# Opening of a two-layer adaptive FFN kernel: bias as two fp32r products, a subtraction on GpSimd, an earlier load, conversions behind additions, one low rank product sooner

## The reference, cut to what matters

```python
att = softmax(gelu(gelu(cond @ W0 + b0) @ W1 + b1) @ W2 + b2)      # 64 x 8
agg_w = einsum('bk,koi->boi', att, weight)                         # 64 x 32 x 32
agg_b = att @ bias_k                                               # 64 x 32
c = einsum('boi,bih->boh', agg_w, x) + agg_b[:, :, None]

def qlinear(x, q, scale, A, Bm):
    w = (q - 7.5) * (scale * 0.005)[:, None]
    return x @ w.T + 0.02 * (x @ A @ Bm)                           # A: 512 x 32, Bm: 32 x 1376
h = silu(qlinear(c, gate...)) * qlinear(c, up...)
x = x + qlinear(h, down...)
x = x + ffn_fp8(conv(x) + context)
```

## Time and profile before

| | us |
|---|---|
| median of three runs | 390.03 (390.01 to 390.49) |
| the profiled execution | 390.28 |
| its span, first to last instruction | 388.4 |
| TensorE busy | 376.7 (97%) |
| VectorE busy | 253.5 (65%) |
| ScalarE busy | 167.6 (43%) |
| GpSimd busy | 80.1 (21%) |

### The profile page before, as it was taken

One profiled execution on the slowest core, in us unless ns is written; L12 is line 12 of the kernel. 1 busy time (PEld: TensorE's weight loads), 2 busy tenths in 40 slices (PEclk: granted clock), 3 DMA queues, 4 the chain that ended last, 5 costly groups with the idle time before them and its releaser, 6 DMA issues.

```text
span 388.4 us, 5833 instructions
## 1 busy us (share of the span) xinstructions
PE 376.7 (97%) x2249; PEld 310.2 (80%) x2249; DVE 253.5 (65%) x406; ACT 167.6 (43%) x304; POOL 80.1 (21%) x67
## 2 busy tenths in 40 slices
PE   7999999999999999999999999999999999999894
PEld 3776877899888888998888789988888899996341
DVE  2659888827376665363766653647889732697994
ACT  6436698402255553022555540225666500254122
POOL 2001422411123223111233231112332312000000
PEclk9699999999999999999999999999999999999999
DMA  6798564199320000222200002254000499974235
GB/s 217 251 278 278 176 217 163 31 323 183 45 43 0 0 2 1 41 42 40 42 0 3 1 0 42 42 70 119 2 0 1 127 294 226 167 187 86 83 136 218
DMA packets 81964, 40.53 MB, mean 104 GB/s; under 512 B 52344, under 2 KB 72840, under 8 KB 81808
## 3 DMA queue, kind: packets, MB, share of 16 engines
q1 hardware_dynamic: 69280, 37.80, 37.0%
q10 hardware_dynamic: 12480, 1.56, 2.7%
q0 software_dynamic: 176, 0.79, 0.6%
HBM read 26.38 MB, written 13.75 MB: 103 GB/s over the span
## 4 chain that ended last, share of the span: by engine, by line
PE 82%; ACT 7%; DVE 7%; issue 2%; POOL 1%; DVEq 0%; ACTq 0%
PE ps L605 34%; PE ps L594 21%; PE ps L541 4%; PE ps L615 4%; PE ps L636 4%; PE ps L770 3%; PE ps L750 2%; PE ps L670 2%; PE ps L638 2%; PE ps L550 1%; DVE y_buf L1102 1%; ACT a_buf L894 1%; ACT mix L834 1%; ACT b_buf L897 1%; PE ps L502 1%
## 5 line engine op out<-in xcount | busy, mean ns | idle before, releaser
L963 POOL TENSOR_TENSOR h_lo<-a_buf,h_hi 128x512 fp32r<-128x512 f32 (+1 forms) x44 | 57.5, 1307 | 126.4 <-ACT h_hi L867 126.4
L594 PE MATMUL ps<-down_w,h_hi 128*128 128x288 f32 (+1 forms) x352 | 76.9, 300 | 0.4 <-DVE down_w L1021 0.3
L594 PE MATMUL ps<-down_w,h_lo 128*128 128x288 f32 (+1 forms) x352 | 74.8, 294 | 0.0
L605 PE MATMUL ps<-x_hi,gate_w 128*128 128x512 f32 (+1 forms) x176 | 70.0, 398 | 0.1
L605 PE MATMUL ps<-x_hi,up_w 128*128 128x512 f32 (+1 forms) x176 | 69.7, 396 | 0.1
L605 PE MATMUL ps<-x_lo,gate_w 128*128 128x512 f32 (+1 forms) x176 | 69.5, 395 | 0.0
L605 PE MATMUL ps<-x_lo,up_w 128*128 128x512 f32 (+1 forms) x176 | 69.3, 394 | 0.0
L1229 DVE TENSOR_TENSOR a_buf<-a_buf,b_buf 128x512 f32<-128x512 f32 (+1 forms) x44 | 54.2, 1233 | 11.6 <-ACT a_buf L908 9.8
L594 PEld LDWEIGHTS ps<-down_w,h_hi 128*128 128x128 f32 (+1 forms) x352 | 57.3, 189 | 1.9 <-issue 0.8
L594 PEld LDWEIGHTS ps<-down_w,h_lo 128*128 128x128 f32 (+1 forms) x352 | 56.2, 188 | 0.0
L1224 DVE TENSOR_TENSOR b_buf<-ps,b_buf 128x512 f32<-128x512 f32 (+1 forms) x44 | 30.2, 686 | 18.9 <-ACT b_buf L897 14.6
(11 more groups left out here) (172 smaller groups left out, 454.6 us busy)
## 6 DMA issues: line engine op xcount, KB each, us to landing
x_nat<-in_x SPq DMA_DIRECT2D x4, 1024.0 KB, 7.7
out<-x_nat SPq DMA_DIRECT2D x16, 256.0 KB, 2.2
turned<-x_nat SPq DMA_DIRECT2D x12, 256.0 KB, 3.3
x_nat<-in_down_q SPq DMA_DIRECT2D x11, 256.0 KB, 3.0
x_nat<-in_gate_q SPq DMA_DIRECT2D x10, 256.0 KB, 7.1
x_nat<-in_up_q SPq DMA_DIRECT2D x10, 256.0 KB, 8.4
edges<-zeros SPq DMA_DIRECT2D x4, 512.0 KB, 9.6
xt<-turned SPq DMA_DIRECT2D x6, 256.0 KB, 3.7
```

Source lines behind the costliest of these rows:

```text
L594: last = mm(ps[:, 4 + 2 * (j % 2) + m, 0:HALF + R], part[0:k, ic, j * P:(j + 1) * P], down_w[0:k, ic, m, :], start=first, stop=end)
L605: last = mm(ps[0:k, bank(ic, 2 * m), :], w[:, H * ic + c * k:H * ic + (c + 1) * k], part[:, c, :], start=c == 0 and part is x1_hi, stop=c ...
L963: nc.gpsimd.tensor_tensor(h_lo[0:k, ic, :], a_buf[0:k, ic % 2, :], plain(h_hi[0:k, ic, :]), ALU.subtract).then_inc(h_lo_ready, 1)
```

## The change

Five edits, all in the opening and the first tile.

1. The bias product is made of fp32r operands. ScalarE rounds `att_bias` to `att_bias_hi` and the ones to `ones_r`; VectorE makes `att_bias_lo`; TensorE adds two one-pass products in the same bank. The 16 passes for the mixture have one `keep_clock` product among them in place of three, and four in place of one stand ahead of `condition(0)`.
2. The low part of B (128 x 688) is subtracted by GpSimd in place of VectorE.
3. The load of `sel` is issued ahead of SP's wait for the parts of B.
4. The two conversions of each chunk of tile 0 stand behind the two additions.
5. The first low rank product stands ahead of the last feature chunk of the third gate product.

```diff
@@ -133,13 +133,16 @@
         bias_k_sb = sb("bias_k_sb", [EXPERTS, S], F32, early)
         cond_w_sb = sb("cond_w_sb", [EXPERTS, S // OB, P], F32, early)
         att_bias = sb("att_bias", [EXPERTS, TILE // S, S], F32, early)
+        att_bias_hi = sb("att_bias_hi", [EXPERTS, TILE], F32R, early)
+        att_bias_lo = sb("att_bias_lo", [EXPERTS, TILE], F32R, early)
+        ones_r = sb("ones_r", [EXPERTS, P], F32R, early)
         stage_lr_a = sb("stage_lr_a", [P, HC, 2, R], F32, early)
         stage_sel = sb("stage_sel", [P, P], F32, early)
         stage_mask = sb("stage_mask", [P, GROUPS + P], F32, early)
         stage_side = sb("stage_side", [P, S], F32, early)
         stage_ctx_w = sb("stage_ctx_w", [P, S], F32, early)
 
-        used = 4 * (COND_COLS + 2 * B + 3 * EXPERTS + B + 6 + S + S // OB * P + TILE + HC * 2 * R + P
+        used = 4 * (COND_COLS + 2 * B + 3 * EXPERTS + B + 6 + S + S // OB * P + 3 * TILE + P + HC * 2 * R + P
                     + GROUPS + P + S + S)
         pad_h = sb("pad_h", [P, (4 * IC * TILE - used) // 4 + 32], F32, early)
         stage_lr_b = sb("stage_lr_b", [P, 2, LRC], F32, early)
@@ -222,6 +225,7 @@
         mix_mm = sem("mix_mm")
         mix_ready, mix_saved, mix_rest = sem("mix_ready"), sem("mix_saved"), sem("mix_rest")
 
+        bias_hi, bias_lo = sem("bias_hi"), sem("bias_lo")
         aggb_mm, aggb_ready = sem("aggb_mm"), sem("aggb_ready")
         row_mm, row_ready, row_stored, row_in = sem("row_mm"), sem("row_ready"), sem("row_stored"), sem("row_in")
 
@@ -410,6 +414,7 @@
             sp.dma_start(stage_ctx_w[:], ctx_w).then_inc(ctx_in, 16)
             sp.dma_start(stage_side[:], fside).then_inc(ctx_in, 16)
             sp.dma_start(stage_mask[:], batch_mask).then_inc(ctx_in, 16)
+            sp.dma_start(stage_sel[:], sel_in).then_inc(sel_w_in, 16)
             sp.wait_ge(lrb_hi, 1)
             sp.wait_ge(lrb_ready, 1)
             sp.dma_start(lr_b_rows.rearrange("m v r (c n) -> (r c) m v n", n=LRC),
@@ -422,7 +427,6 @@
                              lr_b_rows.rearrange("m v r n -> (v r) m n")).then_inc(lrb_laid, 16)
             for n in range(6, RING):
                 load_slot(n)
-            sp.dma_start(stage_sel[:], sel_in).then_inc(sel_w_in, 16)
             sp.dma_start(down_sb[:], down_s).then_inc(down_in, 16)
             sp.dma_start(stage_down_a[:].rearrange("p c r -> p (c r)"), down_a).then_inc(down_in, 16)
             sp.dma_start(stage_down_b[:], down_b).then_inc(down_in, 16)
@@ -522,13 +526,14 @@
             pe.wait_ge(mixw_in, 2 * 16)
             for o in range(S // OB):
                 last = mm(ps[:, MIX_BANK, o * B:(o + 1) * B], cond_w_sb[:, o, :], att_t[:], start=True, stop=True)
-                if o % 2 == 1 and o < S // OB - 1:
+                if o == S // OB // 2 - 1:
                     keep_clock(1)
             last.then_inc(mix_mm, 1)
 
-            pe.wait_ge(att_ready, 2)
-            mm(ps[:, BIAS_BANK, :], ones[0:EXPERTS, :], att_bias[:].rearrange("k b s -> k (b s)"),
-               start=True, stop=True).then_inc(aggb_mm, 1)
+            pe.wait_ge(bias_hi, 2)
+            pe.wait_ge(bias_lo, 1)
+            mm(ps[:, BIAS_BANK, :], ones_r[:], att_bias_hi[:], start=True, stop=False)
+            mm(ps[:, BIAS_BANK, :], ones_r[:], att_bias_lo[:], start=False, stop=True).then_inc(aggb_mm, 1)
 
             def condition(t):
 
@@ -647,7 +652,7 @@
                               start=False, stop=True)
                 last.then_inc(conv_mm, 1)
 
-            keep_clock(1)
+            keep_clock(4)
             pe.wait_ge(mix_ready, 2)
             condition(0)
 
@@ -697,7 +702,8 @@
                     pe.wait_ge(y_ready, t * TG - 1)
                 if t == 0:
                     pe.wait_ge(ag_ready, 1)
-                    quantised(0, 2, 0)
+                    for c in range(HC - 1):
+                        quantised_chunk(0, 2, 0, c)
                     pe.wait_ge(lrb_laid, 2 * 16)
                 for m in range(2):
                     if t > 0:
@@ -709,6 +715,8 @@
                     if t == 0 and m == 1:
                         pe.wait_ge(ctx_sum, 1)
                     low_rank(t, 0, m)
+                    if t == 0 and m == 0:
+                        quantised_chunk(0, 2, 0, HC - 1)
                 low_rank(t, 1, 0)
                 low_rank(t, 1, 1)
                 for ic in range(2, IC):
@@ -795,6 +803,9 @@
 
             act.wait_ge(lr_in, 2 * 16)
             activation(lr_a_w[:, :, :, 0, :], stage_lr_a[:], copy).then_inc(lra_hi, 1)
+            act.wait_ge(att_ready, 2)
+            activation(att_bias_hi[:], att_bias[:].rearrange("k b s -> k (b s)"), copy).then_inc(bias_hi, 1)
+            activation(ones_r[:], ones[0:EXPERTS, :], copy).then_inc(bias_hi, 1)
             act.wait_ge(lrb_in, 16)
             activation(lr_b_parts[:, :, 0, :], stage_lr_b[:], copy).then_inc(lrb_hi, 1)
             act.wait_ge(mix_mm, 1)
@@ -952,6 +963,9 @@
         def _(pool):
             nc.gpsimd.memset(mix[:], 0.0).then_inc(mix_zero, 1)
             nc.gpsimd.memset(zeros[:], 0.0).then_inc(zero_set, 1)
+            pool.wait_ge(lrb_hi, 1)
+            nc.gpsimd.tensor_tensor(lr_b_parts[:, :, 1, :], stage_lr_b[:], plain(lr_b_parts[:, :, 0, :]),
+                                    ALU.subtract).then_inc(lrb_ready, 1)
             pool.wait_ge(row_ready, 1)
             nc.gpsimd.dma_start(bias_row, row_sb).then_inc(row_stored, 16)
 
@@ -1004,9 +1018,9 @@
             v.tensor_tensor(lr_a_w[:, :, :, 1, :], stage_lr_a[:], plain(lr_a_w[:, :, :, 0, :]),
                             ALU.subtract).then_inc(lra_ready, 1)
 
-            dve.wait_ge(lrb_hi, 1)
-            v.tensor_tensor(lr_b_parts[:, :, 1, :], stage_lr_b[:], plain(lr_b_parts[:, :, 0, :]),
-                            ALU.subtract).then_inc(lrb_ready, 1)
+            dve.wait_ge(bias_hi, 1)
+            v.tensor_tensor(att_bias_lo[:], att_bias[:].rearrange("k b s -> k (b s)"), plain(att_bias_hi[:]),
+                            ALU.subtract).then_inc(bias_lo, 1)
 
             dve.wait_ge(mix_mm, 1)
             dve.wait_ge(mix_zero, 1)
@@ -1213,15 +1227,15 @@
                         down_b_low()
                     if t == 0 and ic == 5:
                         convolution_low()
-                    if t == 0:
-                        for later in range(EARLY + 2 * ic, EARLY + 2 * ic + 2):
-                            convert(later)
                     dve.wait_ge(ag_ready, n + 1)
                     dve.wait_ge(l_mm, 2 * n + 1)
                     v.tensor_tensor(a, ps[0:k, bank(ic, 1), :], a, ALU.add).then_inc(g_ready, 1)
                     dve.wait_ge(au_ready, n + 1)
                     dve.wait_ge(l_mm, 2 * n + 2)
                     v.tensor_tensor(b, ps[0:k, bank(ic, 3), :], b, ALU.add).then_inc(u_ready, 1)
+                    if t == 0:
+                        for later in range(EARLY + 2 * ic, EARLY + 2 * ic + 2):
+                            convert(later)
                     if t == TILES - 1 and ic == W_SPREAD - 1:
                         largest_of(w_row_mm, bank(W_SPREAD, 1), w_max, w_steps)
                     dve.wait_ge(silu_ready, n + 1)
```

## The result

The changed kernel takes 388.32 us at the median of seven runs (386.68 to 389.31), the kernel before, timed beside it, 390.49 (390.01 to 390.74). The ratio is 0.9948, with a 95% interval of 0.9924 to 0.9971: faster, by 2.2 us. Before's times lie within 0.7 us of each other, those of the change within 2.6. The three at 389.2 to 389.3 have a mean granted clock of 0.989, the two at 387.7 and 388.3 have 0.992 and 0.993, the two at 386.7 have 0.996.

A forecast was written before the change was run, and what follows sets the result against it. TensorE's chain of waits was taken as the bound: 1.8 (opening) + 0.8 (low rank and conversions) + 0.2 (after) = 2.8 us off the profiled 390.28, giving 387.5. With the median 0.25 below that execution, 387.3 us; range 386.1 to 388.9.

The forecast's parts named there:

- Start of the mixing at 12.9: Opening, tile 0: with the matrix ready at about 12.8 us, `condition(0)` starts at 12.9, 0.7 us sooner.
- bias pair: Opening on TensorE: two one-pass fp32r products at 0.24 us each, 0.5 in place of 1.51 us, ending at 11.4.
- End of the mixing at 17.9: End of `condition(0)`: middle taken between 19.39 (clock rises at 18.56) and 16.47 (high throughout), gain 1.8 us.
- the late clock: Rival, opening: the clock comes back as late as before; gain 1.3 us, 388.7 us, chance 0.14.
- the rival in which the clock never falls: Rival, opening: no low clock once the slow bias product is gone; gain 3.8 us, 386.2 us, chance 0.12.
- Four products bring the clock back sooner: Opening: TensorE runs full products from 11.4 us with hardly a hole, so the clock should rise sooner; time not known.
- sel, worth nothing alone, and without it the gain is lost: `sel` load issued at 9.2 us lands by about 16; alone worth nothing, here it lets the opening's 1.8 us through.
- B on GpSimd costs nothing: Opening: B's store goes 1.8 us later, second reading lands by 27.5 at worst, cover 2.4 us, cost nothing.
- Low rank and conversions, 0.8 us: First low rank products, tile 0: up product of the third chunk starts at 31.65 instead of 32.43, gain 0.8 us.
- After that, 0.2 gained of a range of 0.3 gained to 0.5 lost: Rest of tile 0's gate stage: later products of halves on VectorE meet a 0.31 us wait; 0.2 us gained taken.
- the vector engines as the bound: Rival, tile 0: ScalarE does not follow and TensorE waits at `down`; 0 to 0.8 us gained, 389.6 us, chance 0.06.
- B too late: Rival, opening: GpSimd's subtraction ends at 21.2 us, TensorE waits for B; loss some 4 us, 394 us, chance 0.02.

The follow-up runs named there:

- 12 further runs: The changed kernel itself, nothing altered, timed again beside the kernel before: 388.02 us at the median, ratio 0.9937.
- change's second profile: Profile from re-timing the unaltered changed kernel beside the kernel before: span 386.2 us; median of those runs 388.02 us.

## Why the prediction was right, and where it was not

The range (386.1 to 388.9) held the median of 388.32 and the side was right. The gain was 2.2 us and not 2.8, the predicted 387.3 lay 1.0 under the median, and the forecast's own range of 386.7 to 388.0 just missed it. Of that 1.0 us, 0.46 are not the change's: the forecast counted from 390.03, and before took 390.49 when it was timed beside the change. That the median fell into the range is in part luck, since three of seven runs took 389.2 us or more, above the range; one more of them would have put it outside. The median of the 12 further runs (388.02) is inside again. By the steps:

- *Start of the mixing at 12.9.* Right where the low stretch begins after the bias (12.66). Where it begins at 10.28 the start is 13.64, beyond the 13.5 that the prediction named as its bound. The mis-sized terms are the four products of ones, 1.82 us where 1.4 was taken (the prediction's own bound was 4 x 0.54), and the bias pair, 0.97 instead of 0.5: the pair was priced at the full clock and the four near it, and the trace had the low clock for both.
- *End of the mixing at 17.9, a middle between two bounds.* 17.76 and 18.93 in the two profiles. The wrong step was to take the case as one: the prediction gave chances to three courses of the clock as if one of them would be the kernel's, but at least two occur, from one execution to the next, and a third group of times goes with them. No row had said how long the clock would stay low, so that the middle of the two bounds met 17.76 is luck: it stayed low for 3.41 us there, half of before's stretch. The middle group is the forecast (388.0, predicted 387.3), the low group is nearest to the late clock (389.3, predicted 388.7). The group at 0.996 (386.7) takes the time of the rival in which the clock never falls (predicted 386.2). None of its executions was profiled; an estimate from the marks (span 384.9, less 354.5 after U, 4.0 from S to U and 9.9 from the end of the mixing to S) puts the end of its mixing at 16.5, and 3.57 us at the full clock from 12.9 give just that. So the mixing ran at the full clock. Whether the clock never fell there, or fell and rose ahead of the mixing, is not shown: the mean leaves room for 2.7 to 3.5 us at the low clock. Before's four times within 0.5 us had looked like one course. They were not: of before's 67 runs timed in the three later comparisons 24 had a mean clock of 0.992 or more. Twenty of them, at 0.992 and 0.993, were only 0.4 to 0.8 us faster than the rest.
- *Four products bring the clock back sooner.* Right at the median, 1.1 to 1.2 us by the kernels with one and with two, though each comparison alone is small. It works through how often, not how much. By profiles, the three kernels with one product ahead of the mixing (before, before with `sel` early, one product) all have the long low stretch; of the ten profiles with four, three have it, with falls at 10.28, 10.98 and 11.44, and seven the short one, with falls from 11.19 to 12.46.
- *sel, worth nothing alone, and without it the gain is lost.* Right at the median, as far as it goes: alone it gave some 0.5 us in three runs at 0.993. Its loss was under-sized: without it the change is 3 us worse and slower than before.
- *B on GpSimd costs nothing.* Right: the second reading was issued at 17.1 us, before at 17.3, although the store before it went 1.55 later, so it was not late at all. The prediction had expected it 1.8 later. The store landed within 4.2 us where it had taken 5.9, at 16.4 us against 16.5. The copies of the mixture beside GpSimd's subtraction were not held (1.74 us). That agrees with the Trainium skill ("SBUF — State Buffer", "SBUF: two separate sides"), which has only operations with two SBUF inputs or in a two port mode excluded.
- *Low rank and conversions, 0.8 us.* Measured 0.58.
- *After that, 0.2 gained of a range of 0.3 gained to 0.5 lost.* Wrong in sign, inside its range: 0.39 lost. The prediction had seen that the product of halves would be late at the end of the gate stage. It had not seen that the conversions themselves would be: behind the additions they run beside GpSimd's subtraction and take 1.84 us a pair, and the last ones are the down weights that TensorE asks for next. Its reason for a gain was not empty: chunks 1 to 7 gain 0.6, chunks 8 to 10 lose 0.8.

In the change's second profile, the forecast's course, the steps add up to the whole: 1.96 gained ahead of S, 0.60 to U, 0.36 lost after it, 2.2 us of span.

The rivals with the vector engines as the bound and with B too late did not occur. In the kernel before the chain of waits ran mostly through ScalarE, with VectorE and GpSimd between, from 33 to 73 us; with the change it runs through TensorE up to 68 us.

## What to carry to other kernels

Where a kernel's times fall into groups, sort them by the mean granted clock before comparing medians, look in the profiles at where the clock was low, since low clock behind TensorE's last product lowers the mean and costs nothing, and take marks inside the span (here S and U): at the same marks two single profiles told 0.2 us apart, where medians of ten runs could not. The filler products here cost time where they ran at the low clock and outlasted the copies that they stood beside (13.64 against 12.74), and nothing where they did not; what they bought is the share of executions in which the clock is up, and only many runs show that. When work is put behind something urgent, look at the last turn of the loop, where it is itself the urgent work of the next stage: splitting the rule at chunk 8 gave 0.8 us after the mark U, and the fastest median of all.

## What the runs showed of the hardware that I had not expected

The low stretch of the clock in the opening lasted 6.82 to 6.83 us in six of the 14 profiled executions and 3.41 to 3.42 in the other eight, and began between 10.28 and 12.72 us; the same kernel had both (the change: 6.83 and 3.41). A start of the mixing 1.1 us sooner could end it later (12.55 to 19.28 against 13.64 to 18.93). VectorE's conversions from int32, from SBUF to SBUF, took 1.84 us a pair beside a subtraction on GpSimd and 0.75 without, where its copies out of PSUM took 1.74 beside one and 1.73 without.

Two things stay open. Three of before's runs took 392.8 us at a mean clock of 0.997, and five runs of three kernels 387.7 to 388.4 us, not 386.7, at 0.998 and 0.999. Such means leave at most 2.7 us and 1.9 us at the low clock in all (an estimate: the missing share of the mean, doubled, of the span), less than the shortest low stretch seen, so in these executions the opening had no low stretch of a length seen here, and they were still not the fastest. None of these was profiled.
